# Head stacks copied by the DMA queue, gate weights as one full tile, decay exponents in half precision

## What is computed

```python
xn = layernorm(x)
x  = x + mlstm(xn) + ffn(xn)

# mlstm: 8 heads, DQ = 32, DV = 64
q, k, v, o = xn @ Wq.T, xn @ Wk.T, xn @ Wv.T, xn @ Wog.T
i = 15 * tanh((xn @ Wig.T + big) / 15);  f = 15 * tanh((xn @ Wfg.T + bfg) / 15)
# for each token: m_new = max(logsigmoid(f) + m, i); C and n decay by exp(logsigmoid(f) + m - m_new)
#   and take in exp(i - m_new) * k (x) v;  h = q.C / max(|q.n|, exp(-m_new))
y = (sigmoid(o) * headnorm(h)) @ Wout.T

# ffn: hidden 2048
y = (silu(xn @ Wg.T) * (xn @ Wu.T)) @ Wd.T
```

## Time and profile before

| | us |
|---|---|
| median of 3 runs (lowest, highest) | 3277.08 (3275.98, 3279.02) |
| the profiled execution | 3273.61 |
| its span, first to last instruction | 3271.9 |
| PE busy | 3101.0 (95%) |
| DVE busy | 1876.5 (57%) |
| ACT busy | 1116.8 (34%) |
| POOL busy | 768.3 (23%) |

### The profile page before, as it was taken

The page is one execution under the profiler, slowest core; times in us unless marked ns, Lnnn a source line. Parts: engine busy times, 40 slices in busy tenths (PEclk is TensorE's granted clock), DMA queues, the critical chain, the costliest instruction groups (busy, mean ns, idle before and its releaser), DMA issues.

```text
span 3271.9 us, 61574 instructions
## 1 busy us (share of the span) xinstructions
PE 3101.0 (95%) x22408; PEld 2229.5 (68%) x22408; DVE 1876.5 (57%) x4361; ACT 1116.8 (34%) x2142; POOL 768.3 (23%) x1126
## 2 busy tenths in 40 slices
PE   1499999999999999999999999999999999999999
PEld 0377777677776677776677776677776677776676
DVE  5565555565555565555665555655555655555654
ACT  3433333333333333333333333333333333333332
POOL 4322222222222222222222222222222222222122
PEclk9799999999999999999999999999999999999999
DMA  5000000000000000000000000000000000000000
GB/s 213 7 14 7 6 13 13 13 13 6 6 13 13 13 13 6 6 13 13 13 13 6 6 13 13 13 13 6 6 13 13 13 13 6 6 13 13 13 13 6
DMA packets 20333, 51.08 MB, mean 16 GB/s; under 512 B 1506, under 2 KB 1634, under 8 KB 18274
## 3 DMA queue, kind: packets, MB, share of 16 engines
q1 hardware_dynamic: 20322, 50.95, 4.2%
HBM read 34.16 MB, written 16.78 MB: 16 GB/s over the span
## 4 chain that ended last, share of the span: by engine, by line
issue 74%; POOL 21%; PE 2%; ACT 1%; POOLq 1%; DVE 1%; DVEq 0%; ACTq 0%
POOL arena L530 9%; POOL pair_r L520 4%; POOL small L549 3%; POOL arena L540 2%; POOL begun L537 1%; POOL small L430 1%; PE work L1006 0%; PE work L1008 0%; PE work L1007 0%; POOLq L529 0%; POOL parts_u L481 0%; PE acc L1006 0%; DVE parts_d L740 0%; PE acc L1008 0%; PE acc L1007 0%
## 5 line engine op out<-in xcount | busy, mean ns | idle before, releaser
L530 POOL TENSOR_TENSOR arena<-arena 128x256 f16<-128x256 f32 x512 | 348.1, 680 | 1769.9 <-ACT arena L644 1769.9
L879 DVE SCALAR_TENSOR_TENSOR arena<-arena,work 128x256 f32<-128x256 f32 x512 | 215.8, 422 | 634.4 <-ACT arena L640 628.0
L1006 PE MATMUL work<-xt,parts_g 128*128 128x256 f16 x2048 | 558.4, 273 | 0.0
L1007 PE MATMUL work<-xt,parts_g 128*128 128x256 f16 x2048 | 558.3, 273 | 0.0
L1006 PE MATMUL work<-xt,parts_u 128*128 128x256 f16 x2048 | 558.2, 273 | 0.0
L1007 PE MATMUL work<-xt,parts_u 128*128 128x256 f16 x2048 | 558.2, 273 | 0.0
L1008 PE MATMUL work<-xt,parts_u 128*128 128x256 f16 x2048 | 558.2, 273 | 0.0
L1008 PE MATMUL work<-xt,parts_g 128*128 128x256 f16 x2048 | 558.2, 273 | 0.0
L1006 PE MATMUL acc<-parts_d,arena 128*128 128x512 f16 x1024 | 388.8, 380 | 56.6 <-POOL arena L530 56.6
L640 ACT ACTIVATE arena<-work,unscale 128x256 f32<-128x256 f32 x512 | 240.9, 470 | 583.6 <-PE work L1008 581.0
L644 ACT ACTIVATE arena<-arena 128x256 f16<-128x256 f32 x512 | 213.8, 418 | 645.5 <-DVE arena L882 645.5
(11 more groups left out here) (214 smaller groups left out, 5503.9 us busy)
## 6 DMA issues: line engine op xcount, KB each, us to landing
arena<-x_dram SPq DMA_DIRECT2D x33, 512.0 KB, 3.3
out_dram<-arena SPq DMA_DIRECT2D x32, 512.0 KB, 2.8
parts_u<-w_g_dram SPq DMA_DIRECT2D x4, 1024.0 KB, 14.9
parts_d<-w_u_dram SPq DMA_DIRECT2D x4, 1024.0 KB, 22.8
arena<-w_d_dram SPq DMA_DIRECT2D x4, 1024.0 KB, 9.8
arena<-w_qk_dram SPq DMA_DIRECT2D x1, 1024.0 KB, 5.0
arena<-w_v_dram SPq DMA_DIRECT2D x1, 1024.0 KB, 7.0
arena<-w_o_dram SPq DMA_DIRECT2D x1, 1024.0 KB, 9.0
```

Source lines behind the costliest of these rows:

```text
L530: g.tensor_tensor(hh[:, j % HB, 1, :], tt[:, j % 2, :], hh[:, j % HB, 0, :], ALU.subtract).then_inc(h_ready, 1)
L879: own.step(d.scalar_tensor_tensor(out=tt[:, j % 2, :], in0=tt[:, j % 2, :], scalar=1.0, in1=b[:, 0:BLOCK], op0=ALU.add, op1=ALU.mult))
L1006: t.matmul(dst, w[0], a[0], start=first, stop=False, skip_group_check=True)
L1007: t.matmul(dst, w[0], a[1], start=False, stop=False, skip_group_check=True)
```

## The change

Three edits. The 24 slice copies of a block move from DVE to SP's DMA queue: SP waits for DVE's low parts (`qk_split`), issues 24 SBUF to SBUF transfers, each of 32 partitions by 1 KB, and only then comes to the load of the next x. PE's wait at es0 counts 16 for each transfer. The gate weights get 128 columns a k tile, the new 24 being zeros, and both matmuls of a k tile use all 128. The exponent operands `uhl`, `a_hi`, `pair_l` and `pair_r` become half precision; `uu` is split into two half-precision parts.

```diff
-AFTER[0] = ["stack3"]
-DVE_OWN = 58
+DVE_OWN = 56
-        w_gates = sb("parts_gates", [P, KC, G_LOW + GR], F16)
+        w_gates = sb("parts_gates", [P, KC, P], F16)
-        pair_r = sb("pair_r", [P, NH, P], F32R)
-        pair_l = sb("pair_l", [P, BLOCK], F32R)
+        pair_r = sb("pair_r", [P, NH, P], F16)
+        pair_l = sb("pair_l", [P, BLOCK], F16)
-        uhl = at["uhl"].bitcast(F32R)
-        a_hi = at["lf"].bitcast(F32R)
+        uhl = at["uhl"].bitcast(F16)[:, 0:BLOCK]
+        a_hi = at["lf"].bitcast(F16)[:, 0:BLOCK]
...
             with sp.Fori(0, NB) as i:
 
+                sp.wait_ge(qk_split, 2 * (i + 1))
+                for h in range(HG):
+                    rows = slice(h * DQ, (h + 1) * DQ)
+                    for n, (q_part, k_part) in enumerate(((0, 0), (1, 0), (0, 1))):
+                        to_ = slice((h + n) % HG * DQ, ((h + n) % HG + 1) * DQ)
+                        sp.dma_start(qq[to_, :, h, :], qp[rows, q_part, :, :]).then_inc(stacks_ready, 16)
+                        sp.dma_start(kk[to_, :, h, :], kp[rows, k_part, :, :]).then_inc(stacks_ready, 16)
                 sp.wait_ge(res_copied, NCH * (i + 1))
                 sp.dma_start(xin, x_blocks[bass.ds((i + 1) % NB, 1), :, :, :]).then_inc(x_loaded, 16)
...
+            link(g.memset(w_gates[:, :, G_LOW + GR:P], 0.0))
...
-                def stack(h):
-
-                    rows = slice(h * DQ, (h + 1) * DQ)
-                    for n, (q_part, k_part) in enumerate(((0, 0), (1, 0), (0, 1))):
-                        to_ = slice((h + n) % HG * DQ, ((h + n) % HG + 1) * DQ)
-                        d.tensor_copy(qq[to_, :, h, :], qp[rows, q_part, :, :]).then_inc(stacks_ready, 1)
-                        d.tensor_copy(kk[to_, :, h, :], kp[rows, k_part, :, :]).then_inc(stacks_ready, 1)
...
                 dve.wait_ge(qk_hi, 2 * (i + 1))
-                own.step(d.scalar_tensor_tensor(out=qp[:, 1, :, :], in0=qs, scalar=unscale[:, NS + 2:NS + 3],
-                                                in1=qp[:, 0, :, :], op0=ALU.mult, op1=ALU.subtract))
-                own.step(d.scalar_tensor_tensor(out=kp[:, 1, :, :], in0=kf, scalar=unscale[:, NS + 2:NS + 3],
-                                                in1=kp[:, 0, :, :], op0=ALU.mult, op1=ALU.subtract))
-                own.settle(dve, i)
-                stack(0)
-                stack(1)
-                stack(2)
+                d.scalar_tensor_tensor(out=qp[:, 1, :, :], in0=qs, scalar=unscale[:, NS + 2:NS + 3],
+                                       in1=qp[:, 0, :, :], op0=ALU.mult, op1=ALU.subtract).then_inc(qk_split, 1)
+                d.scalar_tensor_tensor(out=kp[:, 1, :, :], in0=kf, scalar=unscale[:, NS + 2:NS + 3],
+                                       in1=kp[:, 0, :, :], op0=ALU.mult, op1=ALU.subtract).then_inc(qk_split, 1)
...
                 for k in range(KC):
-                    t.matmul(bank("gates")[0:G_LOW + GR, 0:BLOCK], w_gates[:, k, :], xt[:, k, 0, :], start=(k == 0),
-                             stop=(k == KC - 1), skip_group_check=True)
-                    mm_ = t.matmul(bank("gates")[0:GR, 0:BLOCK], w_gates[:, k, 0:GR], xt[:, k, 1, :], start=False,
-                                   stop=(k == KC - 1), skip_group_check=True)
+                    for half in range(2):
+                        mm_ = t.matmul(bank("gates")[:, 0:BLOCK], w_gates[:, k, :], xt[:, k, half, :],
+                                       start=(k == 0 and half == 0), stop=(k == KC - 1 and half == 1))
...
-                            pe.wait_ge(stacks_ready, (i + 1) * 6 * HG)
+                            pe.wait_ge(stacks_ready, (i + 1) * 6 * HG * 16)
```

More of the change, by code:

```diff
@@ L319, in mlstm_mlp_kernel @@
         qk_hi = sem("qk_hi")
+        qk_split = sem("qk_split")
         stacks_ready = sem("stacks_ready")
@@ L451, in _ @@
                                      pattern=[[-1, NH]], channel_multiplier=1))
-            link(g.memset(pair_r[:, :, :].bitcast(F32), 0.0))
+            link(g.memset(pair_r[:, :, :], 0.0))
             for first in (64, 96):
-                link(g.affine_select(out=pair_r[:, :, :], in_=pair_r[:, :, :].bitcast(F32),
+                link(g.affine_select(out=pair_r[:, :, :], in_=pair_r[:, :, :],
                                      compare_op=ALU.not_equal, fill=1.0, base=-first,
                                      pattern=[[-1, NH], [0, P]], channel_multiplier=1))
-            link(g.memset(pair_l[:, :].bitcast(F32), 0.0))
-            link(g.memset(pair_l[0:NH, :].bitcast(F32), -1.0))
-            link(g.memset(pair_l[32:32 + NH, :].bitcast(F32), -1.0))
+            link(g.memset(pair_l[:, :], 0.0))
+            link(g.memset(pair_l[0:NH, :], -1.0))
+            link(g.memset(pair_l[32:32 + NH, :], -1.0))
             link(g.memset(own_head[:, :], 0.0))
@@ L490, in _ @@
                 link(g.memset(at[name], 0.0))
-            link(g.memset(uhl.bitcast(F32), 0.0))
+            link(g.memset(uhl, 0.0))
             for r, names in enumerate(ROUNDS):
@@ L520, in pair @@
                     g.tensor_tensor(pair_r[0:GR, :, :],
-                                    uhl[0:GR, c * P:(c + 1) * P].bitcast(F32).unsqueeze(1).broadcast_to((GR, NH, P)),
+                                    uhl[0:GR, c * P:(c + 1) * P].unsqueeze(1).broadcast_to((GR, NH, P)),
                                     diag[0:GR, :].unsqueeze(2).broadcast_to((GR, NH, P)),
@@ L860, in _ @@
                                          ALU.mult))
-                own.step(d.tensor_tensor(uhl[32:32 + NH, :], uu[0:NH, :], uhl[0:NH, :].bitcast(F32), ALU.subtract))
-                d.tensor_tensor(pair_l[96:96 + NH, :], aa[0:NH, :], a_hi[0:NH, :].bitcast(F32),
+                own.step(d.tensor_tensor(uhl[32:32 + NH, :], uu[0:NH, :], uhl[0:NH, :], ALU.subtract))
+                d.tensor_tensor(pair_l[96:96 + NH, :], aa[0:NH, :], a_hi[0:NH, :],
                                 ALU.subtract).then_inc(parts_ready, 1)
                 dve.wait_ge(qk_hi, 2 * (i + 1))
-                own.step(d.scalar_tensor_tensor(out=qp[:, 1, :, :], in0=qs, scalar=unscale[:, NS + 2:NS + 3],
-                                                in1=qp[:, 0, :, :], op0=ALU.mult, op1=ALU.subtract))
-                own.step(d.scalar_tensor_tensor(out=kp[:, 1, :, :], in0=kf, scalar=unscale[:, NS + 2:NS + 3],
-                                                in1=kp[:, 0, :, :], op0=ALU.mult, op1=ALU.subtract))
-                own.settle(dve, i)
-                stack(0)
-                stack(1)
-                stack(2)
+                d.scalar_tensor_tensor(out=qp[:, 1, :, :], in0=qs, scalar=unscale[:, NS + 2:NS + 3],
+                                       in1=qp[:, 0, :, :], op0=ALU.mult, op1=ALU.subtract).then_inc(qk_split, 1)
+                d.scalar_tensor_tensor(out=kp[:, 1, :, :], in0=kf, scalar=unscale[:, NS + 2:NS + 3],
+                                       in1=kp[:, 0, :, :], op0=ALU.mult, op1=ALU.subtract).then_inc(qk_split, 1)
                 for j in range(NJ):
@@ L886, in _ @@
                         k_ = int(step[-1]) if step[-1].isdigit() else 0
-                        if step == "stack3":
-                            stack(3)
-                        elif step == "stats":
+                        if step == "stats":
                             dve.wait_ge(x_loaded, 16 * (i + 2))
```

## The result

The changed kernel takes 3512.9 us (median of 4 runs, 3511.52 to 3515.84) against 3276.62 for the kernel before (4 runs) on the same chip: a ratio of 1.0721, 95% interval 1.0702 to 1.0739. It is 236 us slower, 7.4 us in each of the 32 blocks. The forecast was 3319, the range 3245 to 3395. The side was right, the size far off.

A forecast was written before the change was run, and what follows sets the result against it. PE, busy 95%, was taken to bound the kernel. Gates -29.5, exponents -3, old wait -56.6, new wait +106, clock +27 and block 0's own fall -2 made +42 us, so 3277 to 3319; range 3245 to 3395.

The forecast's parts named there:

- Bound and old wait: PE bounds, busy 95%; its wait ahead of the first down(0), behind DVE's first 18 copies, goes: -56.6 us.
- Gates: PE's eight gate matmuls a block fall from 1.80 to 0.88 us with 128 columns: -29.5 us.
- Exponent operands: Half-precision e matmul on PE saves 0.1 us a block where it follows fp32 transposes: -3 us.
- The new wait: x load behind 24 copies on SP lands late; DVE waits at stats, PE 3.3 us at wbc: +106 us.
- the price of an issue: Time SP takes to issue one copy: taken as 0.47 us, from loads issued back to back at 0.48 to 0.52.
- The clock: PE's clock falls behind the new wait in half the blocks, 16 x 1.7 us: +27 us.
- the sum: All terms of the forecast added for the whole kernel: +42 us, median to 3319 us.
- Rival 3: Issues or landings dearer than any row; at 0.60 an issue PE also waits at es0: about 3445 us; chance 0.10.
- Rival 1: SP's issues are cheap and x isn't late: 3239 us at 0.40 an issue, 3188 at 0.33 and below; chance 0.18.
- the likeliest case: PE's wait for x exceeds the savings: 3284 us (0.455 an issue) to 3375 (0.50, every block falls); chance 0.60.

The follow-up runs named there:

- spread_only: Kernel before with only the order of DVE's copies changed, one head ahead of ffn0's products, the rest later; no DMA: 3233.2 us, ratio 0.9875.
- gates_only: Kernel before with the 128-column gate tile alone: 3274.4 us over 12 runs, ratio 0.9998.
- copies_only: Kernel before with the copies moved to SP alone, gate tile of 104 columns and fp32r exponent operands as before: 3514.4 us, ratio 1.0729.
- spread: Kernel before with 128-column gate tile, half-precision operands and copies left on DVE, head 0 ahead of ffn0's products, others later: 3206.0 us, ratio 0.9790.
- x_first: Changed kernel with SP issuing the load of the next x ahead of the 24 copies: 3230.9 us, ratio 0.9863.
- probe: Kernel before with half-precision exponent operands and, once ahead of the loop, six sets of four transfers to read issue prices: 3274.1 us, one run.
- filled: Changed kernel with 32 extra 512-column matmuls on PE ahead of the wait for wbc: 3432.1 us, ratio 1.0475.
- x_after_18: Changed kernel with the load of the next x issued behind 18 of the 24 copies: 3403.6 us, ratio 1.0386.
- x_after_12: Changed kernel with the load of the next x issued behind 12 of the 24 copies: 3297.0 us, ratio 1.0055.

## Why the prediction was wrong, point by point

- **Bound and old wait**: right. Moving 18 copies from ahead of `ffn0`'s products takes the wait away, by DMA or on DVE (spread_only). But "POOL had nothing to do with it" goes too far. The first of the two low parts that DVE forms ahead of the copies takes 2.49 us in the block of rows 4, the second, of the same shape, 0.74; the first lies beside POOL's `pair_r`:

```profile
1114.86 2.49 DVE L866 SCALAR_TENSOR_TENSOR arena<-arena,unscale 128x512 f16<-128x512 f32 x1
```

In blocks 0 and 2 the first takes 0.75 and the second, which then lies beside `pair_r`, 2.38 and 2.39. In each case one of the two takes 1.7 us more ahead of the copies, about as much as the old wait is long. No run moves `pair_r`, so whether moving it would end the wait as well stays open.

- **Gates**: right as a cost of PE (0.87 us). "It [...] is kept unless PE meets a wait behind it": PE met one in two kernels. Alone it gives nothing (gates_only), and next to the copies nothing (copies_only). It pays in spread, 27 us over spread_only together with the half precision.
- **Exponent operands**: right, 3.9 us for 3.
- **The new wait**: right in kind, place and chain. SP's order puts x behind the copies, DVE waits at stats, PE at wbc. x_first is the proof.
- **The step that failed** is the price of an issue: "Below 0.38 nothing in the trace goes; above 0.52 nothing excludes more. ... so I take 0.47." It is 0.64. 24 x 0.17 = 4.1 us later, and the wait is 250.3 / 32 = 7.8 us, not 3.3: 250 us where the sum had 106. The rows it rested on were all loads of 4-byte elements from DRAM, and for those 0.47 is right: in the probe one starts 0.46 to 0.48 behind the other from the second on. The number was moved to a kind of transfer that the trace did not have, and the upper end of the range was taken from the wrong kind. Whether SBUF as the source or the 2-byte elements make the difference stays open.
- **The clock**: also too small. The sum had 16 falls at 1.7 us, 27 us; filled shows 81. With x issued near the forecast's own time, the kernel took 3404 (x_after_18). The one case in the trace gave the length of a fall as half-speed work of some 3 us; behind the longer waits it is 4.0 (copies_only), 5.5 and 5.7.
- The sum with the measured terms: -29.5 for the gates, -56.6 and -2 for the old wait, -4 for the operands, +250 for the new wait, +81 for the clock come to +239, against 236 measured.
- Rival 3 named this case (0.60 an issue, 3445) with a chance of 0.10, with too small a clock term and with a second wait at es0 that did not come: the copies had landed before x. Rival 1 leaned on the lone issue of 0.38. In the upper end of the likeliest case the wait at 0.50 an issue is 32 x 4.0 = 129, not 135, which changes nothing here. The Trainium skill's "usually small relative to the DMA itself" (DMA: Bandwidth & Descriptors, Issuing engines are not separate DMA queues) did not hold here: one issue is 0.64 us against 1.9 from issue to landing, a third of it, and 24 in a row take 15 us.

## What to carry to other kernels

Moving small copies from an engine to a DMA queue exchanges their run time for issue time, here 0.3 us for 0.64, and puts them ahead of whatever that queue does next. Look for the load behind them first, and issue it first. Before that, see whether the work may simply run later on its own engine: with the two other edits in both, the copies spread on DVE gave ratios of 0.979 and 0.970, the DMAs with x in front 0.986. Price an operation from a row of the same kind (both ends of a transfer and its type), or widen the range where there is none. And on PE, count a wait with what the clock takes behind it.

## What the runs showed of the hardware

An issue on SP costs 0.62 to 0.67 us from SBUF to SBUF with 2-byte elements and 0.43 to 0.45 from DRAM with 4-byte elements, the mean of four in a row (probe). It is so for 32 and 128 partitions, and from SBUF for rows of 1 KB whole or in two pieces. End and type were not taken apart.

The clock of PE does not need a long wait to fall, and the length of the wait alone does not decide. With a wait of 1.75 us a block the clock stays up (a block at 1.00), with 1.3 too (x_first, mean 0.991). With a single wait of 1.77 at another place of the block it fell (x_after_12), and with 2.0 in 24 of 31 blocks but not in the other 7 (gates_only). With 4.0 and with 7.7 it fell in each. What a fall costs is 1.7 us a block at waits of 2.0 (99.4 against 97.7), some 2.8 at 4.0 (x_after_18), 2.0 at 7.5 (copies_only) and 2.6 at 7.7 (105.8 against 103.2 with the wait filled): more than behind the short waits, but not most behind the longest.

Where the clock fell in every block, the blocks took 99.0, 102.4 and 105.8 us, the last in three kernels that differ in their gates or in the layout of the targets. A saving inside such a block may not show; what ties the times to these steps stays open.
